# A two-batch fusion block: two residuals added by TensorE, one norm scaled by ScalarE, four projections moved ahead

## What is computed

```python
x = x + L0_xattn(layernorm(x), ctx, Wq, ..., W1, b1, W2, b2)   # h = relu(out @ W1 + b1); h @ W2 + b2
x = x + L0_attn(layernorm(x), ...)
x = x + L0_ffn(layernorm(x), ...)
# inside L0_attn:
h = layernorm(x, ln1_g, ln1_b)
h = h + mamba_mixer(rmsnorm(h, rms_w), ...)     # in_proj, conv, x_proj, dt, scan, gate, out_proj
x = x + h
h2 = layernorm(x, ln2_g, ln2_b)
x = x + (relu(h2 @ ffn_w1 + ffn_b1) @ ffn_w2 + ffn_b2)
# inside mamba_mixer:
xi, z = split(x @ in_proj_w); xc = silu(conv(xi) + conv_b)
delta = softplus(...); h_t = exp(delta_t * A) * h_(t-1) + delta_t * xc_t * B_t
y = (sum_n C_t h_t + D * xc) * silu(z);  return y @ out_proj_w
```

## Time and profile before

| | before |
|---|---|
| time, median of 3 | 2993.48 us (2992.93 to 2994.23) |
| the profiled execution | 2994.06 us, its span 2992.3 us |
| PE busy | 2901.6 us (97%) |
| DVE busy | 2204.6 us (74%) |
| ACT busy | 1673.2 us (56%) |
| POOL busy | 2045.0 us (68%) |
| chain that ended last | PE 92%, DVE 6%, ACT 1% |

### The profile page before, as it was taken

The page is one execution under the profiler, slowest core; times in us unless marked ns, Lnnn a source line. Parts: engine busy times, 40 slices in busy tenths (PEclk is TensorE's granted clock), DMA queues, the critical chain, the costliest instruction groups (busy, mean ns, idle before and its releaser), DMA issues.

```text
span 2992.3 us, 41476 instructions
## 1 busy us (share of the span) xinstructions
PE 2901.6 (97%) x14776; PEld 1826.5 (61%) x14776; DVE 2204.6 (74%) x3294; ACT 1673.2 (56%) x2958; POOL 2045.0 (68%) x761
## 2 busy tenths in 40 slices
PE   7999999999999999999999999999999887999999
PEld 4666666666666666666666666666544333445587
DVE  7777777777777777777777777777646899987653
ACT  2567666666767666666666666666623465422021
POOL 1599999999999999999999999999930000002000
PEclk9999999999999999999999999999989988999999
DMA  5544444444445445443444454444350112215100
GB/s 162 143 92 107 103 112 103 100 110 101 111 92 122 99 121 140 110 112 89 115 105 104 100 111 108 92 115 100 70 184 29 42 43 99 85 56 170 71 15 18
DMA packets 145760, 296.26 MB, mean 99 GB/s; under 512 B 36050, under 2 KB 41170, under 8 KB 135986
## 3 DMA queue, kind: packets, MB, share of 16 engines
q1 hardware_dynamic: 135908, 226.76, 27.6%
q0 software_dynamic: 9072, 66.06, 11.8%
q10 hardware_dynamic: 576, 0.79, 0.1%
HBM read 114.47 MB, written 8.06 MB: 41 GB/s over the span
## 4 chain that ended last, share of the span: by engine, by line
PE 92%; DVE 6%; ACT 1%; issue 1%; POOL 0%; DMA 0%; SPq 0%; DVEq 0%; POOLq 0%; ACTq 0%
PE ps L1908 17%; PE ps L1934 16%; PE ps L1947 15%; PE ps L1860 10%; PE ps L1884 9%; PE ps L1891 9%; PE ps L2166 4%; PE ps L2130 3%; PE ps L2146 3%; PE ps L1964 2%; PE ps L1916 1%; DVE bx L1344 1%; DVE pm L1082 1%; PE ps L2158 1%; DVE stats L978 0%
## 5 line engine op out<-in xcount | busy, mean ns | idle before, releaser
L1082 DVE TENSOR_REDUCE pm<-ps 128x1 f32<-128x512 f32 x2048 | 1403.2, 691 | 535.3 <-PE ps L1908 453.6
L1579 ACT ACTIVATE pf<-ps 128x512 f32<-128x512 f32 x2048 | 1203.8, 603 | 654.1 <-PE ps L1934 571.0
L925 POOL TENSOR_TENSOR psum<-psum,pf 128x2048 f32<-128x2048 f32 x317 | 1456.2, 4594 | 18.7
L1908 PE MATMUL ps<-ks,qs 96*128 96x512 f32 x2048 | 832.8, 407 | 8.1 <-DVE pm L1082 3.8
L1934 PE MATMUL ps<-qs,ks 98*128 98x512 f32 x2048 | 814.7, 399 | 1.6 <-ACT pf L1579 1.5
L1908 PEld LDWEIGHTS ps<-ks,qs 96*128 96x128 f32 x2048 | 386.5, 189 | 195.5 <-issue 105.4
L1947 PE MATMUL ps<-pf,V 128*32 128x512 f32 x4096 | 472.5, 602 | 0.0
L1934 PEld LDWEIGHTS ps<-qs,ks 98*128 98x128 f32 x2048 | 391.5, 191 | 46.1 <-ACT pf L1579 12.6
L940 POOL TENSOR_TENSOR ring_r<-ring,w_hi 128x512 fp32r<-128x512 f32 x16 | 21.8, 1373 | 550.7 <-ACT w_hi L1815 550.7
L925 POOL TENSOR_TENSOR psum<-pf 128x2048 f32<-128x2048 f32 x64 | 308.9, 4827 | 50.6 <-ACT pf L1579 50.6
L1884 PE MATMUL ps<-cTh,Wkg 128*128 128x512 f32 x732 | 300.8, 411 | 1.0 <-POOL cTl L889 1.0
(11 more groups left out here) (237 smaller groups left out, 3041.8 us busy)
## 6 DMA issues: line engine op xcount, KB each, us to landing
ks<-KH SPq DMA_DIRECT2D x1024, 64.0 KB, 2.0
psum<-pf POOLq DMA_DIRECT2D x63, 1024.0 KB, 8.6
ks<-KL SPq DMA_DIRECT2D x512, 64.0 KB, 2.0
cT<-in_ctxT SPq DMA_DIRECT2D x32, 768.0 KB, 6.0
Wkg<-wk_rows SPq DMA_DIRECT2D x61, 384.0 KB, 3.0
BC<-bc_rows SPq DMA_DIRECT2D x32, 512.0 KB, 4.8
ring<-in_ffn_w SPq DMA_DIRECT2D x16, 1024.0 KB, 8.1
wA<-in_W_fcT SPq DMA_DIRECT2D x4, 1024.0 KB, 11.4
```

What stands on the lines that cost most here:

```text
L925: pool.tensor_tensor(acc, before, pf[:, tile % P_SLOTS, :], ALU.add).then_inc(s_sum, 1)
L1082: dve.tensor_reduce(pm[:, of % 2, n // BLK, n % BLK:n % BLK + 1], src, AX.X, ALU.max).then_inc(s_wfree, 1)
L1579: act.activation(pf[:, tile % P_SLOTS, j * NTOK:(j + 1) * NTOK], ps[:, S_BANK + u % S_BANKS, :], ACT.Exp, scale=SCALE).then_inc(s_exp, 1)
L1908: last = pe.matmul(dst, qs[0:3 * HD, h, t * P:(t + 1) * P], ks[0:3 * HD, keys_of(of, j), i * 512:(i + 1) * 512], start=True, stop=True)
```

## The change

1. **b1's residual on TensorE.** `second_product(1, t)` begins with a ninth block, the identity times x_res; ScalarE copies the sum out (`with_residual`), and VectorE, which used to add, only waits for the copy. A semaphore s_bias lets TensorE wait for b2 having been added to x_res.
2. **b1's rms norm on ScalarE.** VectorE only makes the reciprocal root (s_rms); ScalarE multiplies by it, and rms_w is applied when the transposed tiles are copied out, in 16 activations (`turned_scaled`) for 4 copies.
3. **b0's mixing.** `mix(0, t)` begins with a fifth block, identity times xa; ScalarE copies out, VectorE waits for the copy.
4. **Order.** xw1(1, 4 to 7) goes ahead of xz(0, 6) and xz(0, 7) on TensorE and in the banks, and ScalarE's `gated(0, 2)`, `gated(0, 3)` go from step 1 to step 4.

```diff
@@ SEGMENTS
-     + stage(0, "xz")[6:] + stage(1, "xw1")[AHEAD_1:]),
+     + stage(1, "xw1")[AHEAD_1:] + stage(0, "xz")[6:]),
@@ vector: half_norm
-                        unit_ready(dve, w)
-                        empties(dve.tensor_tensor(x_res[b][:, k, :], x_res[b][:, k, :], bank(w), ALU.add), w)
+                        if b == 0:
+                            unit_ready(dve, w)
+                            empties(dve.tensor_tensor(x_res[b][:, k, :], x_res[b][:, k, :], bank(w), ALU.add), w)
+                        else:
+                            unit_emptied(dve, w)
...
-                    if k > 0:
+                    if k > 0 and b == 0:
                         normalise(b, k - 1, var_of[b, k - 1, "hr"], hr[b], tn[b], m1b[:, 3, :], rms=True,
                                   signal=s_norm[b])
+                    elif k > 0:
+                        root = std[b][:, k - 1:k]
+                        dve.wait_ge(s_std[b], var_of[b, k - 1, "hr"])
+                        dve.reciprocal(root, root).then_inc(s_rms, 1)
@@ vector: mixed
-                unit_ready(dve, w)
-                empties(dve.tensor_tensor(xa[b][:, t, :], xa[b][:, t, :], bank(w), ALU.add), w)
+                if b == 0:
+                    unit_emptied(dve, w)
+                else:
+                    unit_ready(dve, w)
+                    empties(dve.tensor_tensor(xa[b][:, t, :], xa[b][:, t, :], bank(w), ALU.add), w)
@@ scalar
+            def with_residual(w, dst):
+
+                unit_ready(act, w)
+                act.copy(dst[:, w[2], :], bank(w)).then_inc(s_free[UNIT_BANK[w]], 1)
...
                 k, second = divmod(h, 2)
+                if b == 1 and k < NT and not second:
+                    with_residual((b, "xw2", k), x_res[b])
...
+                if b == 1 and k > 0 and second:
+                    act.wait_ge(s_rms, k)
+                    act.activation(tn[b][:, k - 1, :], hr[b][:, k - 1, :], ACT.Identity, scale=std[b][:, k - 1:k]
+                                   ).then_inc(s_norm[b], 1)
...
                     act.wait_ge(s_hr, NB)
-                    turned(1, "rms_T", tT[1])
+                    act.wait_ge(s_norm[1], 3 * NT)
+                    turned_scaled(1, "rms_T", "rms_w")
...
                 if LN2_0 <= j < LN2_0 + NT // 2:
+                    for t in range(2):
+                        with_residual((0, "mix_out", 2 * (j - LN2_0) + t), xa[0])
                     for t in range(2):
                         root(0, 2 * (j - LN2_0) + t)
...
                 if j == 1:
                     hidden(1, range(AHEAD_1, F1 // P))
+                if j == S_SLOTS:
                     for f in range(KD // 2, KD):
                         gated(0, f)
@@ tensor: second_product, mix, order ahead of the loop
-                product((b, "xw2", t), [(xhid[:, f, t * P:(t + 1) * P], xw2[:, f, :]) for f in range(F1 // P)])
+                residual = [(ident[:], x_res[b][:, t, :])] if b == 1 else []
+                product((b, "xw2", t), residual + [(xhid[:, f, t * P:(t + 1) * P], xw2[:, f, :])
+                                                   for f in range(F1 // P)])
...
+                residual = [(ident[:], xa[b][:, t, :])] if b == 0 else []
+                product((b, "mix_out", t), residual + [(zs[b][:, f, t * P:(t + 1) * P], w_out[:, f, :])
+                                                       for f in range(KD)])
...
             dt_of(0)
+            first_product(1, range(AHEAD_1, F1 // P))
             xz(0, 6)
             xz(0, 7)
-            first_product(1, range(AHEAD_1, F1 // P))
```

More of the change, by code:

```diff
@@ L367, in emit @@
         s_hr = sem("s_hr")
+        s_bias = sem("s_bias")
+        s_rms = sem("s_rms")
         s_shift = sem("s_shift")
@@ L405, in emit @@
                      ("dt_b", KD), ("Dp", KD), ("ffn_b1", F2 // P), ("b_fc", F2 // P), ("ln2_g", KD),
-                     ("ln2_b", KD), ("eps", 1)):
+                     ("ln2_b", KD), ("rms_w", KD), ("eps", 1)):
             COL[n] = (at, k)
@@ L1194, in with_bias @@
                     last = dve.tensor_tensor(x_res[b][:, t, :], x_res[b][:, t, :], m1b[:, 0, :], ALU.add)
-                link(last)
+                last.then_inc(s_bias, 1)
+                dve.wait_ge(s_bias, b + 1)
             def add_norm(b):
@@ L1648, in normal, with turned_scaled @@
                                bias=msq[b][:, t:t + 1]).then_inc(s_norm[b], 1)
-            def turned_scaled(b):
+            def turned_scaled(b, stage, gain, shift=None):
                 for t in range(NT):
-                    w = (b, "ln2_T", t)
+                    w = (b, stage, t)
                     unit_ready(act, w)
@@ L1656, in turned_scaled @@
                         last = act.activation(tT[b][:, k, t * P:(t + 1) * P], bank(w)[:, k * P:(k + 1) * P],
-                                              ACT.Identity, scale=col("ln2_g", k), bias=col("ln2_b", k))
+                                              ACT.Identity, scale=col(gain, k), bias=col(shift, k) if shift else 0.0)
                     last.then_inc(s_free[UNIT_BANK[w]], 1)
@@ L1765, in beside @@
                 if j == TURN_2 + 1:
-                    turned_scaled(0)
+                    turned_scaled(0, "ln2_T", "ln2_g", "ln2_b")
                 if LN2_0 <= j < LN2_0 + NT // 2:
+                    for t in range(2):
+                        with_residual((0, "mix_out", 2 * (j - LN2_0) + t), xa[0])
                     for t in range(2):
@@ L2060, in second_product @@
                     unit_emptied(pe, (b, "xw1", F1 // P - 1))
-                product((b, "xw2", t), [(xhid[:, f, t * P:(t + 1) * P], xw2[:, f, :]) for f in range(F1 // P)])
+                    if b == 1:
+                        pe.wait_ge(s_bias, NB)
+                residual = [(ident[:], x_res[b][:, t, :])] if b == 1 else []
+                product((b, "xw2", t), residual + [(xhid[:, f, t * P:(t + 1) * P], xw2[:, f, :])
+                                                   for f in range(F1 // P)])
             def xz(b, m):
@@ L2098, in mix @@
                     if b == 0:
+                        pe.wait_ge(s_hr, 1)
                         pe.wait_ge(s_w["outp"], 16)
-                product((b, "mix_out", t), [(zs[b][:, f, t * P:(t + 1) * P], w_out[:, f, :]) for f in range(KD)])
+                residual = [(ident[:], xa[b][:, t, :])] if b == 0 else []
+                product((b, "mix_out", t), residual + [(zs[b][:, f, t * P:(t + 1) * P], w_out[:, f, :])
+                                                       for f in range(KD)])
             def up(b, m):
@@ L2291 @@
                                  columns(arr("L0_attn_ffn_b1")), columns(arr("L0_ffn_b_fc")),
-                                 columns(arr("L0_attn_ln2_g")), columns(arr("L0_attn_ln2_b"))], axis=1),
+                                 columns(arr("L0_attn_ln2_g")), columns(arr("L0_attn_ln2_b")),
+                                 columns(arr("L0_attn_rms_w"))], axis=1),
         "m1b": spread(arr("L0_xattn_b2"), arr("L0_attn_ln1_g"), arr("L0_attn_ln1_b"),
```

## The result

| | before | after |
|---|---|---|
| time, median of 17 runs each | 2993.96 us (2991.20 to 2996.37) | 2999.78 us (2995.09 to 3002.19) |
| ratio | 1 | 1.002, 95% interval 1.0013 to 1.0027 |
| profiled execution, its span | 2992.3 us | 2995.2 us |

The change makes the kernel 5.8 us slower. By the 95% interval of the ratio it is between 3.9 and 8.1 us. The forecast was +9.2 us, 3002.7 us, with a range of 2998.8 to 3007.0: the measured time lies 1 us inside its lower end, and the size that was forecast lies outside the interval.

A forecast was written before the change was run, and what follows sets the result against it. Two full TensorE stretches, opened by y_sum(11) and up(0, 0), were taken to bound the kernel. +5.8 us at the first (+11.0 less 5.2) and +3.4 from b0's mixing made +9.2: 3002.7 us, range 2998.8 to 3007.0.

The forecast's parts named there:

- The bound: Two full TensorE stretches, begun by y_sum(11) and up(0, 0): what moves their starts moves the end by as much.
- Rivals A and D: A: first step size not delayed, 2989.0 us, 7%; D: that with b0's mixing cost hidden too, 2985.6 us, 3%.
- The first statistics: Start of VectorE's statistics for b1's norm, after xw2's first product and ScalarE's copy: forecast at 2356.65.
- scan 2's wait in before: VectorE's 3.70 us wait for dA, laid to ScalarE standing at the xw1 products before dA(2).
- The hazard of the table load: Root's table load behind tile 0's copy: 0.1 to 0.2 us showing; by the skill's draining 1.4 us more.
- their cover: ScalarE's 16 pieces, 5.71 us, run during VectorE's steps 10 and 11, done some 3 us before xz(1, 0).
- The start of y_sum(11): Opening of the first full stretch: +11.0 less 5.2 gives +5.8 us, bounds +4.5 and +9.
- the shift is carried on unaltered from there: From y_sum(11) to y_sum(32) nothing changes, so the +5.8 us is passed on whole.
- Rival B: b0's mixing cost is hidden: +5.8 us alone, 2999.3 us, 10%.
- rival C: Lower clock through xw2's first product, or VectorE waiting for copies at tiles 1 to 3: 3006.5 us, 10%.
- The sum: Whole kernel: 5.8 + 3.4 = +9.2 us on the profiled execution, predicted median 3002.7 us.

The follow-up runs named there:

- the order alone: Kernel before with only the four xw1 products ahead of xz(0, 6) and xz(0, 7), and two gates at step 4: 3005.34 us, ratio 1.0037.
- half the products: Kernel after with two of the four xw1 products moved back behind xz(0, 7): 2991.22 us, ratio 0.9997.
- the other deal of the banks: Against before: parts 1 and 2, gates at step 4, xz(0, 6) and xz(0, 7) in banks 6, 7, xw1 in 3, 4, 5, 0: 2984.69 us.
- three profiles of before: The unedited kernel before, profiled first and then twice more; the repeats took 2992.7 and 2995.29 us.
- the seven profiles above: Profiles of kernels unchanged from before up to y_sum(0), which took 1.98 or 1.99 us three times and 2.84 to 3.48 four times.
- +3.33 alone: Kernel before with only b0's mixing changed (identity block, ScalarE copies out): 2996.93 us, ratio 1.0011.
- the second and third profile of after: The kernel after repeated with no edit, twice more: 3000.49 and 3002.5 us.
- the fourteen profiles: All profiles of this case: before and after three times each, and eight other kernels once each; the kernels' times ran from 2984.69 to 3005.34 us.

## Why the prediction was right, step by step

**The bound.** Right. Both full stretches hand every shift on: in the order alone, 9.77 at scan 3 is 9.79 at y_sum(37).

**Part 4.** Right to the hundredth at its root: 13.74 us forecast for the first step size, 13.74 found in after and in the order alone, 6.88 with half the products. Rivals A and D are out with it. y_sum(0) starts 8.30 us later (2344.21 forecast, 2307.64 + 36.71 = 2344.35 found). The first statistics were forecast at 2356.65, 49.0 behind the dbc copy; they stand at 49.5, 48.7 and 48.7. One reading was wrong, without weight in the sum: scan 2's wait in before was laid to the xw1 products, and it was for the gates, as the other deal of the banks showed.

**Part 1.** The three later tiles save 0.7 each, and the copies never hold VectorE up at them (its statistics rows of tiles 1 to 3 show no idle time), as forecast. The hazard of the table load: behind the copy it stands indeed (2354.54, 1.28 us), the root follows directly, and VectorE waits 0.51 us for it instead of 0.36 as before: 0.15, the estimate from the row. By the draining that the Trainium skill adds to a load (ScalarE: Activation LUTs, What ACT_TABLE_LOAD costs) it would have been 1.5, an estimate from the page's 1.38; the trace doesn't show it:

```profile
2353.93 0.59 ACT L1704 COPY x_res<-ps 128x512 f32<-128x512 f32 x1 [8.18 <-PE ps L1888]
2354.54 1.28 ACT L1541 ACT_TABLE_LOAD   x1
2355.83 0.29 ACT L1541 ACTIVATE std<-msq,cols 128x1 f32<-128x1 f32 x1
```

**Part 2.** Right, 5.4 us for parts 1 and 2 together from scan 3 to scan 11 in after (+11.65 to +6.28) and 5.2 forecast. The 16 pieces took 4.20 us here, not 5.71 as those with a shift per feature, so their cover was wider than thought.

**The start of y_sum(11).** +5.8 forecast; +6.28, +5.43 and +5.47 found. Up to here the sum holds.

**What failed: that the shift is carried on unaltered from there.** The forecast took "y_sum(11), and the first full stretch, start at +5.8" as one thing. But in before y_sum(11) and the first record of xz(1, 0) behind it ran at the lower clock, and in after at the full one, so y_sum(12) is 2.25 us less late than y_sum(11):

```profile
2414.92 3.78 PE L2146 MATMUL ps<-bx,ident 128*128 128x512 f32 x4 [0.72 <-DVE bx L1350]
2418.49 4.09 PE L1860 MATMUL ps<-tT,w_in 128*128 128x512 f32 x8
```
```profile
2418.59 1.98 PE L2181 MATMUL ps<-bx,ident 128*128 128x512 f32 x4 [0.72 <-DVE bx L1363]
2420.41 3.60 PE L1888 MATMUL ps<-tT,w_in 128*128 128x512 f32 x8
```

I had priced the clock only where the change makes TensorE wait longer, at y_sum(0), and not where it was low already and could come back. That is the largest part of the 3.4 us by which the forecast was too high. The others change from one execution to the next and show in the mean: in one of three profiles of before the first stretch is 1.5 us longer by a slow start at y_sum(0), and in one of three of after up(0, 0) is 1.7 us faster: 0.5 and 0.6 us. By the seven profiles above, of which four have the slow start, the first would be 0.8 rather than 0.5, an estimate.

**Part 3.** Right: +3.4 forecast, +3.33 alone, +3.4 in the second and third profile of after (from y_sum(32), +3.17 and +3.22, to scan 35, +6.56 and +6.62), +3.8 in the first, where TensorE was 0.3 us longer at the lower clock in front of the first block. Rival B, that it is hidden, is out; so is rival C in its main term: xw2's first product ran at the full clock, but for its identity block in the first profile.

**The sum.** 9.2 - 2.25 - 0.5 - 0.6 = 5.9, for 5.8 measured. Mechanism, sign and places were right, and one term, the clock at y_sum(11), was missing. That the range held the result without it owes something to luck: its lower part stood for rival B, that part 3 is hidden, which isn't what happened.

**What stays open.** Why part 1 gives y_sum(11) the full clock. It isn't the pause in front of y_sum(10). Part 1 adds a block to each of four products, so TensorE does more in the 73 us ahead (2345.28 to 2418.59), but no run here isolates that from where the records fall. Filler products between the transposes and y_sum(10) would test it; that wasn't tried.

## What to carry to other kernels

A product moved ahead of another delays whoever waits for the other, for whatever reason it waits: here not for the result but for the memory under the product's input, in a line that the change didn't touch. Before moving work on an engine's queue, list the waits on every unit that it is moved past. And what such a move is meant to give may be had another way: the stalls were one behind the gates in ScalarE's queue and one for a bank, and later gates with another deal of the banks, TensorE's order kept, took both away at no price that the run shows (2984.69 us with parts 1 and 2, 9.1 below before).

Work taken off a busy engine is worth its time only where that engine is what the next full stretch waits for: the add taken off VectorE saved 2.18 us over three tiles of b1's norm, where TensorE had room, against 0.86 for the block of the first tile; it cost 3.3 us in b0's mixing, where VectorE was waiting for TensorE and the block fell on TensorE.

## What the hardware showed that I had not expected

A TensorE at 0.50 of its clock can be a term of the sum at every place where a full stretch begins, not just where a pause grows: y_sum(11) took 3.78 us in six profiles of six without part 1 and 1.98 in eight of eight with it, 2.25 us on the path; the blocks that go with it stand 35 to 73 us earlier. At other places the same program differs from run to run: scan 3 of the kernel before 1.48 us later in one profile of three, up(0, 0) 3.70 or 5.40 us. The copy of dbc, behind the attention, starts up to 5.2 us apart among the fourteen profiles, as much as the 17 timed runs of before spread (2991.2 to 2996.4), and a difference of a few us is only to be understood from a common anchor.
